# Values ahead of scores, projections and a feed-forward chunk moved into the loop, a new order at the end

## The chip, the core and the metric

One core of a Trainium2 chip runs the kernel, written instruction by instruction for each engine: TensorE (PE, matrix products), VectorE (DVE), ScalarE (ACT), GpSimd (POOL), and SyncE (SP), which here only issues DMA transfers. Each engine works through its own list in the order in which the program wrote it, and waits at semaphores for the others. The metric is the time of one execution on the device in microseconds (us), lower is better.

## The reference

Two sequences of 1024 tokens of 128 values go through one layer: local attention, a layer norm, a feed-forward block with ternary weights, a layer norm.

```python
qkv = xp @ w_qkv                       # 16 heads of 64; q scaled by 1/8
# token 0 ("bos") is a key of every query; its own output is its value row
# the other tokens stand in blocks of 16; a block of queries sees 5 blocks of
# keys (two before, itself, two behind), minus those that lie behind the query
sim  = einsum('bhnid,bhnjd->bhnij', qw, kw); sim = where(mask, -max, sim)
attn = softmax(sim)
attn = einsum('gh,bhnij->bgnij', w_th, attn)        # mixes the 16 heads
out  = einsum('bhnij,bhnjd->bhnid', attn, vw) ... @ w_out + b_out
x = layernorm(x + out)
h = gelu(ternary(w_up) applied to x / rms(x))       # 128 -> 512
x = layernorm(x + ternary(w_down) applied to h / rms(h))   # 512 -> 128
```

As the mask leaves only keys at or before the query, three blocks matter, so a query block has 50 keys: 3 x 17 less one.

## The kernel before

**Layout.** The 2 x 1024 tokens are cut into 8 chunks of 256 tokens. A chunk takes four slots of the main loop, `for s in range(STEPS)` with 32 slots, and each engine has its own copy of that loop. The weights were combined ahead, so that a query part is a product with the head's own matrix `Gh`/`Gl`, and the way out a product with `Mh`/`Ml`. A number of full precision is carried as a rounded high half and the rest, a low half (names ending in h and l, or high and low): ScalarE makes the high half, VectorE (or GpSimd) subtracts to get the low one, and three products (`split3`, L1106 to L1110) stand for one.

**The attention of a slot.** `queries(s, 0)` and `queries(s, 1)` (TensorE, 6 products of 256 columns each) make queries for the chunk ahead; ScalarE copies them out (`y_out`). `scores(s)` makes eight tiles of 50 keys (64 small products and a mask product). VectorE takes the maximum and subtracts it (`shift`), ScalarE makes the exponential, VectorE the sum and its reciprocal (`total`), GpSimd multiplies (`normalise`, L519). `transposes(s)` turns the result on TensorE, ScalarE and VectorE copy it out (`at_hi`, `at_lo`), `c_part(s)` multiplies by the values (12 products, L1257), `ct_hi` and `ct_lo` copy that out. `o_part(n, p)` is the projection of chunk n, in four parts of 12 products. In slot s the order on TensorE is: transposes(s-2), scores(s), pieces of feed-forward, queries(s, 0), one projection part (that of slot s-7), queries(s, 1), c_part(s-2). The lag of two slots is `LAG`, that of seven `O_LAG`.

**The feed-forward block** of chunk n is spread over slots by `ffn(s)`, which gives pairs (n, k) with k = s - FIRST[n], and FIRST[n] = 11 + 4n. k = -1: `stage` (ScalarE adds the bias to the attention's output); 0: `attn_back`, `residual`, `variance_roots`; 1: `input_scale`, `up_input`, `x1_T`, `x1_hi`; 2: `x1_lo`, `up`, `gelu`; 3: `hidden_high`; 4: `hidden_low` (GpSimd, L533), `squares`, `down`, `down_out`; 5: `down_back`, `square_sum`, `hidden_root`, `second_sum`; 6: `second_norm`, `last_root`; 7: `result_shift`; 8: `result`. Chunks 0 to 3 run so. Chunk 4 is in the loop up to `up` (at k = 4), and chunk 5 up to `attn_back`. All that is left stands behind the loop, in an order written out by hand for each engine, with the scores' last pieces, the projections of chunks 6 and 7, and the feed-forward work of chunks 4 to 7. `keep_busy(bank, count)` issues products whose result nobody reads.

**The window rows.** The values of a chunk are read from DRAM into `raw` by SP (`window`, 6 to 11 transfers). GpSimd rounds them into the high half (`rows_high(c)`, L502, waits until all of chunk c have landed) and subtracts for the low one (`rows_low`, L506), after which SP may overwrite `raw` with the next chunk's. In GpSimd's loop:

```python
for n, k in ffn(s):
    if k == 4 and n < 4: hidden_low(n, 0); hidden_low(n, 1)
    if k == 5: hidden_root(n)
normalise(s)
... # k == 0: variance_roots(n); k == 6: last_root(n)
if s % 4 == 1 and s < STEPS - 4: rows_high((s + 3) // 4)
if s % 4 == 0 and s > 0:         rows_low(s // 4)
```

## Time and profile before

| | |
|---|---|
| time, median of 3 runs | 241.5 us (241.25 to 242.36) |
| the profiled execution | 243.09 us, of it 241.3 us span of the profile |
| PE busy | 226.1 us, 94% of the span |
| DVE busy | 176.6 us, 73% |
| ACT busy | 164.1 us, 68% |
| POOL busy | 92.6 us, 38% |
| mean DMA traffic | 48 GB/s |
| granted PE clock | 9 tenths or more of full speed, in the last two of 40 slices 7 and 5 |

Busy time of an engine is the time in which it works on any instruction. Products overlap in the array, so the time of one (about 0.28 us) is more than its distance to the next (0.12 us); distances are read from start to start. In a row of a timeline stand the start and the duration in us, the engine, the line of the kernel, the operation, the output and input tiles with their sizes, how many instructions were merged, and in brackets how long the engine had been idle before and whom it waited for.

### The profile page before, as it was taken

The page shows a single profiled execution, that of the slowest core. Times are in us where ns is not written, and L with a number is a line of the kernel's source. Part 1 is how long each engine was busy: PE and PEld are TensorE (multiplying, and loading weights), DVE is VectorE, ACT ScalarE, POOL GpSimd, SP SyncE. Part 2 cuts the span into 40 slices and gives each one's busy share as a digit, 9 for nine tenths or more (in the row PEclk, how much of TensorE's full clock was granted, in tenths as well). Part 3 has the DMA queues.
Part 4 walks back from the last instruction along what each step waited for, and adds up shares of the span by engine and source line. Part 5 has one row for each costly group of instructions (what it writes and reads, how often), then busy time and mean ns, then how long its engine had stood idle before and what let it go on. Part 6 is the DMA issues. An engine that isn't in the chain of part 4 may idle for free.

```text
span 241.3 us, 10011 instructions
## 1 busy us (share of the span) xinstructions
PE 226.1 (94%) x4343; PEld 203.1 (84%) x4343; DVE 176.6 (73%) x461; ACT 164.1 (68%) x311; POOL 92.6 (38%) x111
## 2 busy tenths in 40 slices
PE   7999899999999999999999999999999989989970
PEld 7899789888999999888988998888988977889750
DVE  0674699987777882688766885688468999785864
ACT  2686466776666648985599559964898334988652
POOL 7035204531343342444515454536254353120542
PEclk9999999999999999999999999999999999999975
DMA  6937560020020001100200111010201001000002
GB/s 217 293 101 209 165 139 7 7 61 3 3 58 13 24 3 39 35 21 8 65 3 4 48 34 36 3 46 4 68 3 29 20 3 46 1 4 22 3 3 87
DMA packets 19107, 11.69 MB, mean 48 GB/s; under 512 B 2232, under 2 KB 18168, under 8 KB 18936
## 3 DMA queue, kind: packets, MB, share of 16 engines
q1 hardware_dynamic: 18324, 10.47, 15.3%
q8 instruction: 34, 0.56, 1.0%
q10 hardware_dynamic: 740, 0.59, 0.8%
q14 instruction: 9, 0.07, 0.1%
HBM read 8.91 MB, written 2.10 MB: 46 GB/s over the span
## 4 chain that ended last, share of the span: by engine, by line
PE 57%; DVE 15%; ACT 8%; issue 7%; POOL 6%; SPq 2%; DMA 2%; POOLq 0%; DVEq 0%; ACTq 0%
PE bank L1108 9%; PE bank L1110 8%; PE bank L1109 8%; PE bank L1257 7%; PE bank L1231 6%; PE bank L1215 4%; DVE CTl L876 4%; POOL gTl L533 2%; DVE AT L881 2%; POOL xw L506 2%; DMA raw<-in_L_attn_x 2%; SPq L395 2%; DVE sm L896 2%; PE bank L1327 2%; PE bank L1189 2%
## 5 line engine op out<-in xcount | busy, mean ns | idle before, releaser
L577 ACT ACTIVATE Yb<-bank 128x512 f32<-128x512 f32 x64 | 38.4, 601 | 28.4 <-PE bank L1110 27.9
L519 POOL TENSOR_TENSOR E<-E,rc 128x400 f32<-128x400 f32 x32 | 27.9, 871 | 77.3 <-DVE rc L898 77.3
L876 DVE TENSOR_TENSOR CTl<-bank,CTh 128x512 fp32r<-128x512 f32 x64 | 41.1, 683 | 22.3 <-ACT CTh L577 22.1
L1108 PE MATMUL bank<-xTh,Gh 128*128 128x256 f32 x128 | 39.4, 308 | 1.7 <-ACT Yb L577 1.5
L1108 PE MATMUL bank<-CTh,Mh 128*128 128x256 f32 x128 | 37.0, 289 | 0.6 <-DVE CTl L876 0.6
L577 ACT ACTIVATE CTh<-bank 128x512 fp32r<-128x512 f32 x64 | 34.8, 600 | 2.5 <-PE bank L1257 2.4
L1110 PE MATMUL bank<-CTh,Ml 128*128 128x256 f32 x128 | 36.1, 282 | 0.0
L724 ACT ACTIVATE E<-E 128x400 f32<-128x400 f32 x32 | 17.3, 541 | 27.5 <-DVE E L890 27.4
L1109 PE MATMUL bank<-CTl,Mh 128*128 128x256 f32 x128 | 36.0, 281 | 0.0
L1109 PE MATMUL bank<-xTl,Gh 128*128 128x256 f32 x128 | 35.8, 280 | 0.0
L1110 PE MATMUL bank<-xTh,Gl 128*128 128x256 f32 x128 | 35.7, 279 | 0.0
L1257 PE MATMUL bank<-AT,xw 50*128 50x256 f32 x384 | 31.1, 294 | 0.8 <-DVE AT L881 0.7
L1231 PE MATMUL bank<-xT,Yb 128*32 128x50 f32 x2048 | 29.9, 209 | 1.1 <-issue 1.1
L1231 PEld LDWEIGHTS bank<-xT,Yb 128*32 128x32 f32 x2048 | 25.2, 109 | 6.7 <-issue 6.4
L1257 PEld LDWEIGHTS bank<-AT,xw 50*128 50x128 f32 x384 | 24.6, 185 | 5.3 <-DVE AT L881 1.4
L896 DVE TENSOR_REDUCE sm<-E 128x8 f32<-128x400 f32 x32 | 18.2, 570 | 13.5 <-ACT E L724 13.4
L1108 PEld LDWEIGHTS bank<-xTh,Gh 128*128 128x128 f32 x128 | 24.3, 190 | 3.4 <-ACT Yb L577 2.3
L1108 PEld LDWEIGHTS bank<-CTh,Mh 128*128 128x128 f32 x128 | 24.1, 188 | 0.9 <-DVE CTl L876 0.9
L1109 PEld LDWEIGHTS bank<-xTl,Gh 128*128 128x128 f32 x128 | 24.2, 189 | 0.0
L1109 PEld LDWEIGHTS bank<-CTl,Mh 128*128 128x128 f32 x128 | 24.1, 189 | 0.0
L1110 PEld LDWEIGHTS bank<-xTh,Gl 128*128 128x128 f32 x128 | 24.1, 188 | 0.0
L1110 PEld LDWEIGHTS bank<-CTh,Ml 128*128 128x128 f32 x128 | 24.0, 188 | 0.0
(142 smaller groups left out, 469.3 us busy)
## 6 DMA issues: line engine op xcount, KB each, us to landing
raw<-in_L_attn_x SPq DMA_DIRECT2D x37, 64.0 KB
pt_rows<-PT SPq DMA_DIRECT2D x2, 512.0 KB, 4.7
R<-pt_rows SPq DMA_DIRECT2D x1, 1024.0 KB, 5.6
xr<-in_L_attn_x SPq DMA_DIRECT2D x6, 128.0 KB
out<-y SPq DMA_DIRECT2D x6, 128.0 KB, 1.9
raw<-in_L_attn_x SPq DMA_DIRECT2D x13, 56.0 KB
w_sb<-in_L_attn_w_qkv SPq DMA_DIRECT2D x2, 256.0 KB, 4.7
w_sb<-in_L_attn_w_qkv ACTq DMA_DIRECT2D x2, 256.0 KB, 4.5
```

The source lines that it names most:

```text
L395: sp.dma_start(raw[own, first:last, :], src[0:BLK]).then_inc(s_raw, 16)
L519: tt(e, e, rc[s % 2][:, :].unsqueeze(2).broadcast_to([P, TILES, WIN]), ALU.mult).then_inc(s_norm, 1)
L577: copy = lambda o, i, **k: nc.scalar.activation(o, i, ACT.Copy, **k)
L724: nc.scalar.activation(e, e, ACT.Exp).then_inc(s_exp, 1)
L876: v.tensor_tensor(ct_view(CTl[s // 4 % 2], s % 4, q), c_view(s, q), ct_view(f32(CTh[s // 4 % 2][:, :, :]), s % 4, q), ALU.subtract).then_i ...
L896: v.tensor_reduce(sm[k][:, :], E[k][:, :, 0:WIN], AX.X, ALU.add).then_inc(s_sum, 1)
L1108: mm(o, wh, rh, start=start, stop=False, **k)
L1109: mm(o, wh, rl, start=False, stop=False, **k)
L1110: return mm(o, wl, rh, start=False, stop=stop, **k)
L1215: ins = nc.tensor.transpose(o[:, :, IL * f:IL * f + IL], E[s % 2][:, k:k + 2, :].rearrange("p t w -> p (t w)"), ident[:, :])
L1231: mm(bank[S_BANK][lo:lo + 32, WIN * tile:WIN * tile + WIN], Yb[s // 4 % 2][:, ytile, lo:lo + 32], keys, start=(tile == 0), stop=False, ski ...
L1257: ins.append(mm(c_bank(s, q)[:, col], xw[s // 4 % 2][row, m, c, :], AT[row, a, col], start=(n == 0), stop=(n == 2)))
```

## The change

Six things, in all engines' lists:

1. From slot 8 on TensorE begins a slot with c_part(s-2), then scores(s), then transposes(s-1), one slot sooner than before. ScalarE and VectorE copy in that order. Slot 7 (`TURN`) is the slot in which the order turns.
2. O_LAG is 6: projection parts come one slot sooner. Slot 7 has two of them, and slot 31 too.
3. FIRST[n] is 10 + 4n for all chunks of the loop: every feed-forward stage of chunks 0 to 4 comes one slot sooner. The window rows keep their slots.
4. The square sums of a chunk stand inside the scores' block. Gelu stands ahead of the second query copy on ScalarE.
5. Chunk 4 runs in the loop up to second_sum, and its hidden_low is done by GpSimd and no longer by VectorE.
6. The lists behind the loop are new, and there are 30 idle products in place of 5.

```diff
@@ -56,7 +56,8 @@
...
 LAG = 2
-O_LAG = 7
+O_LAG = 6
+TURN = 7
 NT = B * N // P
...
@@ -279,19 +280,20 @@
...
-    if s < 28:
-        return [divmod(s - O_LAG, 4)] if s >= O_LAG else []
-    return {28: [(5, 1), (5, 2)], 29: [(5, 3)], 30: [(6, 0)], 31: []}[s]
-FIRST = [11 + 4 * n for n in range(5)] + [30]
+    if s < TURN:
+        return []
+    early = {7: [(0, 0), (0, 1)], 31: [(6, 1), (6, 2)]}
+    return early.get(s, [divmod(s - O_LAG, 4)])
+FIRST = [10 + 4 * n for n in range(6)]
...
-    return [(n, s - first) for n, first in enumerate(FIRST) if -1 <= s - first < (9, 9, 9, 9, 5, 1)[n]]
-UP_BANK = {5: (0, 2), 6: (0, 2), 7: (6, 5)}
+    return [(n, s - first) for n, first in enumerate(FIRST) if -1 <= s - first < (9, 9, 9, 9, 6, 1)[n]]
+UP_BANK = {5: (1, 0), 6: (2, 0), 7: (6, 5)}
 AT_BANK = {7: 5}
-XT_BANK = {5: 4, 7: 5}
+XT_BANK = {5: 2, 7: 5}
 DN_BANK = {5: 4, 6: 3, 7: 0}
...
@@ -309,14 +311,11 @@
...
-def c_bank(s, q):
-    return bank[(0, 2)[q] if s == 30 else C_BANK[q]]
 def y_bank(s, b):
...
 def squared(n):
-    return gT[0] if n < 4 else gT[2] if n % 2 else gsq
+    return gT[0] if n < 5 else gT[2] if n % 2 else gsq
...
@@ -343,7 +342,7 @@
...
 def c_view(s, q):
-    return c_bank(s, q)[:, :].rearrange("p (r h s) -> p r h s", r=2, s=BLK)
+    return bank[C_BANK[q]][:, :].rearrange("p (r h s) -> p r h s", r=2, s=BLK)
...
@@ -545,7 +544,7 @@
...
         for n, k in ffn(s):
-            if k == 4 and n < 4:
+            if k == 4:
                 hidden_low(n, 0)
...
@@ -561,11 +560,10 @@
...
+    last_root(4)
     variance_roots(6)
     variance_roots(7)
-    hidden_root(4)
     hidden_root(5)
-    last_root(4)
     hidden_root(6)
...
@@ -679,11 +677,11 @@
...
         o = slice(2 * t, 2 * t + 2)
-        if n < 4:
+        if n < 5:
             act.wait_ge(f_gl, 2 * n + t + 1)
...
             act.wait_ge(f_gl, 12)
-        elif n > 5:
+        elif n > 6:
             act.wait_ge(f_ss, n - 1)
...
@@ -705,24 +703,33 @@
...
             act.wait_ge(s_small, 32)
-        if s > LAG:
+        if LAG < s <= TURN:
             ct_hi(s - LAG - 1)
-        if 0 < s < O_LAG:
+        if 0 < s < TURN:
             y_out(s, 0)
-        if s >= LAG:
+        if LAG <= s <= TURN:
             at_hi(s - LAG)
-        if s == 0 or s >= O_LAG:
+        if s == 0 or s == TURN:
             y_out(s, 0)
-        if s < O_LAG:
+        if s >= TURN:
+            ct_hi(s - 2)
+            at_hi(s - 1)
+        if s > TURN:
+            y_out(s, 0)
+        if s < TURN:
             y_out(s, 1)
         for n, k in ffn(s):
-            if k == 4 and n < 4:
+            if k == 4:
                 squares(n, 0)
...
         nc.scalar.activation(e, e, ACT.Exp).then_inc(s_exp, 1)
-        if s >= O_LAG:
+        for n, k in ffn(s):
+            if k == 2:
+                gelu(n, 0)
+                gelu(n, 1)
+        if s >= TURN:
             y_out(s, 1)
...
@@ -730,46 +737,34 @@
...
         for n, k in ffn(s):
-            if k == 4 and n < 4:
+            if k == 4:
                 down_out(n)
...
                 x1_hi(n)
-            if k == 3 and n < 4:
+            if k == 3:
                 hidden_high(n, 0)
                 hidden_high(n, 1)
-            if k == 2 and n < 4:
-                gelu(n, 0)
-                gelu(n, 1)
-            if k == 8 and n < 3:
+            if k == 8:
                 result(n)
-    at_hi(30)
-    ct_hi(29)
-    gelu(4, 0)
+    x1_hi(5)
+    ct_hi(30)
     at_hi(31)
-    ct_hi(30)
-    gelu(4, 1)
+    stage(6)
     ct_hi(31)
-    x1_hi(5)
-    stage(6)
-    hidden_high(4, 0)
-    hidden_high(4, 1)
-    squares(4, 0)
-    squares(4, 1)
     gelu(5, 0)
...
     hidden_high(5, 1)
-    result(3)
     x1_hi(6)
+    result(4)
     squares(5, 0)
     stage(7)
+    squares(5, 1)
     gelu(6, 0)
...
     hidden_high(6, 1)
-    down_out(4)
-    squares(5, 1)
     down_out(5)
...
@@ -782,7 +777,6 @@
...
     down_out(7)
-    result(4)
     result(5)
...
@@ -1005,27 +999,25 @@
...
             dve.wait_ge(s_pt, 32)
-        if s > LAG:
+        if LAG < s <= TURN:
             ct_lo(s - LAG - 1)
-        if s >= LAG:
+        if LAG <= s <= TURN:
             at_lo(s - LAG)
+        if s > TURN:
+            ct_lo(s - 2)
+        shift(s)
+        if s == TURN:
+            ct_lo(s - 2)
         for n, k in ffn(s):
-            if k == 5 and n == 3:
+            if k == 5:
+                dve.wait_ge(f_back, n + 1)
                 hidden_sum(n)
+        if s >= TURN:
+            at_lo(s - 1)
         for n, k in ffn(s):
...
                 up_input(n)
-        shift(s)
-        for n, k in ffn(s):
-            if k == 5 and n < 3:
-                hidden_sum(n)
-            if k == 5 and n == 3:
-                second_sum(n)
-            if k == 6 and n == 3:
-                second_norm(n)
-            if k == 0 and n == 5:
-                residual(n)
         if s == STEPS - 1:
...
@@ -1035,11 +1027,11 @@
...
             ternary(0)
-        if 4 <= s < O_LAG:
+        if 4 <= s < TURN:
             fills(IN_STEP[s - 1][-1:])
...
         for n, k in ffn(s):
-            if k == 5 and n < 3:
+            if k == 5:
                 second_sum(n)
...
@@ -1055,45 +1047,39 @@
...
         for n, k in ffn(s):
-            if k == 0 and n < 5:
+            if k == 0:
                 residual(n)
-            if k == 6 and n < 3:
+            if k == 6:
                 second_norm(n)
-    at_lo(30)
-    ct_lo(29)
+    x1_lo(5)
+    ct_lo(30)
     at_lo(31)
-    ct_lo(30)
+    second_norm(4)
     ct_lo(31)
-    x1_lo(5)
     residual(6)
-    hidden_low(4, 0)
-    hidden_low(4, 1)
+    result_shift(4)
+    hidden_low(5, 0)
     input_scale(6)
     up_input(6)
-    hidden_low(5, 0)
     hidden_low(5, 1)
...
     input_scale(7)
-    hidden_sum(4)
     up_input(7)
-    second_sum(4)
+    hidden_sum(5)
     x1_lo(7)
-    hidden_sum(5)
-    second_norm(4)
     second_sum(5)
+    second_norm(5)
     hidden_sum(6)
     hidden_low(7, 0)
-    second_norm(5)
     hidden_low(7, 1)
-    result_shift(4)
     second_sum(6)
+    result_shift(5)
     hidden_sum(7)
     second_norm(6)
-    result_shift(5)
     second_sum(7)
...
@@ -1216,7 +1202,7 @@
...
-    def scores(s):
+    def scores(s, sums=()):
...
@@ -1230,6 +1216,9 @@
...
                    start=(tile == 0), stop=False, skip_group_check=True)
+        for n in sums:
+            pe.wait_ge(f_dS, n + 1)
+            square_sum(n)
         if s % (2 * SLOTS) == 0:
...
@@ -1242,10 +1231,7 @@
...
         pe.wait_ge(s_ATl, s + 1)
-        need(pe, s_CTl, 60 if s == 31 else 2 * s if s < 30 else 0)
-        if s == 30:
-            pe.wait_ge(s_sub, STEPS)
-            pe.wait_ge(s_Ye, 64)
+        need(pe, s_CTl, 2 * s)
         if s % 4 == 0:
...
@@ -1254,7 +1240,7 @@
...
                     row = slice(64 * q, 64 * q + WIN)
-                    ins.append(mm(c_bank(s, q)[:, col], xw[s // 4 % 2][row, m, c, :], AT[row, a, col],
+                    ins.append(mm(bank[C_BANK[q]][:, col], xw[s // 4 % 2][row, m, c, :], AT[row, a, col],
                                   start=(n == 0), stop=(n == 2)))
...
@@ -1272,10 +1258,8 @@
...
         pe.wait_ge(f_stage, n + 1)
-        if n < 5:
+        if n < 6:
             need(pe, f_gelu, 2 * n)
-        elif n == 6:
-            pe.wait_ge(f_gelu, 10)
         for i in range(CT):
...
@@ -1288,12 +1272,10 @@
...
-        if n < 5 and t == 0:
+        if n < 6 and t == 0:
             need(pe, f_y2, CT * n)
-        if n == 4 and t == 1:
-            pe.wait_ge(f_res, 6)
-        if n == 6:
-            pe.wait_ge(f_gelu, 11 + t)
+        if n == 6 and t == 1:
+            pe.wait_ge(f_gelu, 12)
         pe.wait_ge(f_xTl, n + 1)
...
@@ -1342,14 +1324,18 @@
...
     for s in range(STEPS):
-        if 0 < s < O_LAG:
+        if 0 < s < TURN:
             queries(s, 0)
...
             pe.wait_ge(s_evd, read_no("D", "p", 3))
-        if s >= LAG:
+        if LAG <= s <= TURN:
             transposes(s - LAG)
-        scores(s)
+        if s > TURN:
+            c_part(s - 2)
+        scores(s, [n for n, k in ffn(s) if k == 5])
+        if s > TURN:
+            transposes(s - 1)
         if s == FIRST[0]:
...
@@ -1358,21 +1344,21 @@
...
                 attn_back(n)
-            if k == 2 and n < 4 or k == 4 and n == 4:
+            if k == 2:
                 up(n, 0)
                 up(n, 1)
-        if s == 0 or s >= O_LAG:
+        if s == 0 or s >= TURN:
             queries(s, 0)
-        for n, k in ffn(s):
-            if k == 5:
-                square_sum(n)
-        if s == O_LAG:
+        if s == TURN:
             pe.wait_ge(s_eva, read_no("A", "m", 3))
...
             o_part(*part)
+            if part == (0, 0):
+                c_part(s - 2)
+                transposes(s - 1)
         for n, k in ffn(s):
-            if k == 4 and n < 4:
+            if k == 4:
                 down(n)
...
@@ -1380,41 +1366,38 @@
...
             fills(IN_STEP[s])
-        if s >= LAG:
+        if LAG <= s < TURN:
             c_part(s - LAG)
-    transposes(30)
-    o_part(6, 1)
+    x1_T(5)
     c_part(30)
     transposes(31)
-    o_part(6, 2)
+    o_part(6, 3)
     c_part(31)
-    x1_T(5)
-    o_part(6, 3)
+    up(5, 0)
+    up(5, 1)
     attn_back(6)
     o_part(7, 0)
-    up(5, 0)
-    up(5, 1)
     o_part(7, 1)
...
     up(6, 1)
+    down(5)
     attn_back(7)
-    down(4)
-    down(5)
-    down_back(4)
-    square_sum(4)
+    down_back(5)
+    square_sum(5)
+    keep_busy(1, 4)
     down(6)
-    down_back(5)
+    square_sum(6)
+    keep_busy(1, 4)
     x1_T(7)
-    square_sum(5)
     down_back(6)
+    keep_busy(1, 6)
     up(7, 0)
     up(7, 1)
-    square_sum(6)
-    keep_busy(2, 5)
+    keep_busy(1, 16)
     down(7)
...
```

## Rows read from the trace of the kernel before

**Rows 1.** Timeline of TensorE (PE), slots 14 and 15: start us, us, engine, line, operation, tiles.

```profile
97.65 0.38 PE L1108 MATMUL bank<-xTh,Gh 128*128 128x256 f32 x1 [0.36 <-ACT Yb L577]
...
98.55 0.97 PE L1257 MATMUL bank<-AT,xw 50*128 50x256 f32 x12
99.45 0.65 PE L1215 MATMUL bank<-ident,E 128*128 128x128 f32 x4
...
101.89 0.28 PE L1108 MATMUL bank<-CTh,Mh 128*128 128x256 f32 x1
...
103.32 0.28 PE L1309 MATMUL bank<-gTh,wdT 128*128 128x256 f32 x1
...
104.05 0.38 PE L1309 MATMUL bank<-gTh,wdT 128*128 128x256 f32 x1
```

**Rows 2.** Timeline of TensorE: scores(12), scores(28), the last values part.

```profile
82.06 0.92 PE L1231 MATMUL bank<-xT,Yb 128*32 128x50 f32 x64
...
185.08 0.92 PE L1231 MATMUL bank<-xT,Yb 128*32 128x50 f32 x64
...
209.61 0.98 PE L1257 MATMUL bank<-AT,xw 50*128 50x256 f32 x12
```

**Rows 3.** Timeline of TensorE at the end.

```profile
220.19 0.28 PE L1301 MATMUL bank<-x1Th,wuT 128*128 128x256 f32 x1
...
223.68 0.71 PE L1327 MATMUL bank<-ones,gsq 128*32 128x1 f32 x64
...
227.09 0.39 PE L1301 MATMUL bank<-x1Th,wuT 128*128 128x256 f32 x1
...
232.19 0.58 PE L1309 MATMUL bank<-gTh,wdT 128*128 128x256 f32 x1 [0.75 <-DVE gTl L949]
```

**Rows 4.** Busy time by stretches: us, then each engine, PEclk the granted clock.

```profile
230.00:241.30 11.30, 4.14 (x79) 3.10 (x78) 6.31 (x34) 4.25 (x10) 4.27 (x5) 0.58 0.16 48
```

**Rows 5.** Timeline of GpSimd (POOL), windows of chunks 4, 5 and 7.

```profile
87.76 0.86 POOL L519 TENSOR_TENSOR E<-E,rc 128x400 f32<-128x400 f32 x1 [4.27 <-DVE rc L898]
88.58 2.40 POOL L506 TENSOR_TENSOR xw<-raw,xw 114x1024 fp32r<-114x1024 f32 x1
...
99.62 1.04 POOL L502 CAST xw<-raw 114x1024 fp32r<-114x1024 f32 x1 [6.17 <-PE bank L1257]
...
101.45 2.55 POOL L533 TENSOR_TENSOR gTl<-gT,gTh 128x512 fp32r<-128x512 f32 x2
...
114.04 2.40 POOL L506 TENSOR_TENSOR xw<-raw,xw 114x1024 fp32r<-114x1024 f32 x1
...
119.77 0.69 POOL L544 TENSOR_TENSOR rstd<-var,exps 128x2 f32<-128x2 f32 x1
121.01 1.04 POOL L502 CAST xw<-raw 114x1024 fp32r<-114x1024 f32 x1 [0.55 <-DMA raw<-in_L_attn_x]
...
166.21 2.39 POOL L506 TENSOR_TENSOR xw<-raw,xw 114x1024 fp32r<-114x1024 f32 x1
...
175.10 1.04 POOL L502 CAST xw<-raw 114x1024 fp32r<-114x1024 f32 x1 [2.47 <-DMA raw<-in_L_attn_x]
```

**Rows 6.** Timeline of SyncE's queue, last issue of chunk 4's window.

```profile
97.54 0.70 SPq L398 DMA_DIRECT2D raw<-in_L_attn_x  x1
```

**Rows 7.** Timeline of VectorE (DVE) in a plain slot.

```profile
65.83 1.29 DVE L876 TENSOR_TENSOR CTl<-bank,CTh 128x512 fp32r<-128x512 f32 x2 [1.02 <-ACT CTh L577]
...
68.23 0.57 DVE L890 TENSOR_TENSOR E<-bank,mx 128x400 f32<-128x400 f32 x1
```

**Rows 8.** Timeline of ScalarE (ACT), the Gelu of chunk 0.

```profile
93.25 1.28 ACT L668 ACT_TABLE_LOAD   x1
94.55 1.09 ACT L668 ACTIVATE gT<-bank 128x512 f32<-128x512 f32 x2
```

**Rows 9.** Timeline of VectorE at the end.

```profile
231.44 0.69 DVE L949 TENSOR_TENSOR gTl<-gT,gTh 128x512 fp32r<-128x512 f32 x1
...
235.53 0.16 DVE L961 SCALAR_TENSOR_TENSOR weight<-hroot,ratio 128x2 f32<-128x2 f32 x1
```

## The prediction

> **What bounds the kernel now.** I read the page first. In its 40 slices TensorE shows 8 or 9 tenths everywhere but in the first and the last two. I went on to the waits of TensorE and of GpSimd, then to the timelines of both round one hidden-layer slot, and last to the end. I call one pass of the loop over s a slot, its eight score tiles scores(s), and so on. In the middle nearly everything is TensorE at a steady pace: a product of 256 columns every 0.117 us, 12 of them (one projection part) in 103.32 - 101.89 = 1.43, a values part in 99.45 - 98.55 = 0.90 [rows 1]. A plain slot is values 0.90, scores 0.9, four transposes 0.6 (0.66 with the last one's tail), projection 1.43 and two query parts of 6 products with a wait, 0.8 each: 5.4. Between scores(12) at 82.06 and scores(28) at 185.08 lie 103.02 us, four chunks of 25.8 [rows 2]. The reader is to see the two places in a chunk where TensorE waits: before the second query part of slot 14 (97.65, behind ScalarE's copy, 0.36 idle and about 0.5 between starts), and inside the down product of slot 15 (104.05, 0.26 lost and a slower first product, 0.36 together) [rows 1]. That is 0.9 us a chunk. The end is a chain: the last projection part ends at 220.19 where the products of up(6) start, those of up(7) start at 227.09, and the second half of down(7) at 232.19 has waited for VectorE [rows 3]; in that last stretch the granted clock is 0.58 on the mean [rows 4], so mostly at the lower of its two levels.
>
> **The other thing to see is GpSimd's queue.** GpSimd does three things in program order: normalise(s), the window rows (rows_low at s%4 = 0, rows_high at s%4 = 1), and hidden_low. After rows_low frees the raw buffer, SP issues the next window's transfers, and rows_high waits for the last. For chunk 4: rows_low ends at 88.58 + 2.40 = 90.98, the last issue starts at 97.54, rows_high starts at 99.62, 8.64 after the buffer came free [rows 5, 6]. (The row names a product as releaser, but that count was reached by the values part of slot 13; what is left is the last landing.) For chunk 5 it is 121.01 - 116.44 = 4.57; chunk 6 has as many transfers as 5, I give it the same. For chunk 7 it is 175.10 - 168.60 = 6.50 [rows 5]. None of it hurts before, because hidden_low comes two slots after rows_high's own slot (s = 15 against s = 13): rows_high(4) ends at 100.66, hidden_low starts at 101.45 [rows 5], the down product at 103.32 [rows 1].
>
> **The change, part by part.**
>
> *Work moved ahead.* At scores(28) TensorE has done more than before: one values part 0.90, one projection part 1.43, the transpose back and the square sums of chunk 3 (0.25, two transposes of the kind that take 0.66 in four, and 0.71, as at 223.68 [rows 3]), one x1 transpose with its wait 0.3. Together +3.6 at that point. It is no extra work; what it gives back stands under the end.
>
> *The loop's own waits.* In the new order a values part opens the slot, then come scores, then the transposes of the slot before. The risk is a ring: values, copy on ScalarE, ct_lo, the shift, at_lo on VectorE, next values. A pair of ct_lo takes 1.29, a shift piece 0.57 [rows 7]. I count 0.90 + 0.15 + 0.60 to the first copy's end, two ct_lo 1.2, two shift pieces 1.15, at_lo 0.68: 4.7 us in a slot of 5.4. So the plain slots stay TensorE's, with 0.7 to spare. Gelu in the slot s%4 = 0 now stands before the second query copy: its table load of 1.28 and 1.09 of Gelu [rows 8], and the load back for Exp in the slot after, push normalise(s) of that slot about 0.35 past the transposes. I take 0.35 a chunk, between 0 and 1.0 (the length of ScalarE's slack in either case). So 0.9 is removed and 0.35 put in its place: -0.55 a chunk, -2.2 for four.
>
> The Trainium skill (ScalarE: Activation LUTs, "What ACT_TABLE_LOAD costs") gives a switch of tables about 2.66 us, a drain counted in. Here the load starts at 93.25 and the Gelu at 94.55 [rows 8], so the trace shows 1.28 and no drain; by the page each slot with a load would be 1.4 longer, of which chunks 5 and 6 would feel about 0.35 each.
>
> *Hidden work one slot sooner.* FIRST goes from 11 to 10, so hidden_low(n) falls in the slot right after rows_high's, while rows_low and rows_high keep their slots. On GpSimd it stands behind rows_high, which stands behind a transfer. Count both from the end of normalise(12). TensorE: remaining 0.2, scores 0.9, transposes 0.6, queries 0.8, projection 1.43, queries 0.8; then values 0.9, scores 0.9, the 0.35, transposes 0.6, transpose back of attention 0.15, queries 0.8, projection 1.5: down(0) is wanted at 9.9 and done at 10.85. GpSimd: rows_low 2.40, transfer 8.64, rows_high 1.04, hidden_low 2.55 for two halves [rows 5], then half of down, 0.5: done at 15.1. TensorE is held 4.2. For chunks 5 and 6 last_root, which now stands ahead of rows_low and waits for second_norm, adds 0.85 (0.69 for itself [rows 5]): 0.85 + 2.40 + 4.57 + 1.04 + 2.55 + 0.5 = 11.9, held 1.05 each. For chunk 7, with 6.50: 13.85, held 3.0. Sum +9.3. ScalarE's squares wait for the same halves and Exp behind them, but the values, scores and squares that follow take longer than Exp, total and normalise (about 2.3), so nothing is added. Bounds: with chunk 5's interval in all four the sum is 3.4; if each hold also put one normalise (0.86) on the path it is 12.7. I take 9.3, the rows' own intervals.
>
> *Slots 28 to 31.* Without query parts the ring binds. It costs TensorE nothing where there was idle time before (about 2.4 us between 185 and 210.5), and the new order fills some of that. From scores(28) to the end of the last values part: before 209.61 + 0.9 - 185.08 = 25.4 [rows 2]; after, slot by slot with chunk 4's Gelu, down and squares in it, 25.7. So +0.3, between -1.5 and +2.5.
>
> *The end.* The last values part is now followed by up(5) and attn_back(6), which fit in the 2.1 us that the last ct_lo needs; before, the third part of chunk 6, held up behind it, made that 2.7, and up(5) stood inside the last projections: -1.55 to their end. Then up(6) and the new place of down(5) (0.94) stand before attn_back(7), +0.95. The idle products ahead of x1_T(7) and of up(7) have 4 and 6 of 0.117; squares and these come after down(6), and up(7) is late by another 1.45. From up(7) on it is the other way: low halves no longer wait for second_norm(5) (the one at 231.44 could be at 230.35, where its high half is done [rows 9]), the last products run at the upper clock, hidden_sum(7) comes 1.95 sooner after up(7), and so does all behind 235.53 [rows 9], less what it waits there for second_norm(6). Sum -1.55 + 0.95 + 1.45 - 2.0 = -1.15. Bounds -3.5 (idle products free) and +0.5.
>
> For the clock the Trainium skill (TensorE: Matmul & The Clock Gate, "Why this matters for your kernels") asks that TensorE not be left idle between bursts. By it the 16 products ahead of down(7) hold the upper level, as my sum has it; if they did not, the last part would be about 0.7 longer.
>
> *Everything else* (banks, squared into gT[0] for chunk 4, the square sums inside the scores block, removed special cases) is the same instructions in other places; the split of chunk 4 goes from VectorE (1.29 a pair) to GpSimd (2.55), in a slot without window rows: 0.
>
> **The sum.** +3.6 - 2.2 + 9.3 + 0.3 - 1.15 = +9.85. Against the profiled execution, 243.09 (span 241.3), that is 252.9; it lay 1.6 above the median 241.5, so for the median 251.3, said as 251.
>
> **Rivals.**
> *Half of the hold.* Landings come sooner, or TensorE is so late for other reasons in these slots that down(n) waits little: only chunk 4's and 7's holds stay, at half size, 3.6 instead of 9.3: 245.6. For it: the rows' intervals depend on SP's issue times (0.25 to 1.3 each), which vary. Against: the order on GpSimd is fixed, and 8.64 was measured. Chance 0.17.
> *Faster.* The hold does not show at all, and the new order takes every wait out of the loop (-3.6) while the end gains its full 3.5: 3.6 - 3.6 - 1.5 - 3.5 = -5 at most; half of that is likelier, 239. It decides if rows_high ends less than 5.4 us after rows_low in each chunk (10.4, when the second half of down is wanted, less 2.55 and 2.40). In the rows it is 9.7 for chunk 4, 5.6 for 5 and 7.5 for 7 (with last_root, 0.85 less is allowed). Chance 0.14.
> *Nothing.* Work and waits only change places; TensorE's products are the same but for 25 idle ones. The moved 3.6 is paid back by the end and the waits: 241.5. Chance 0.07.
> *Worse.* The ring binds in plain slots too, because ScalarE's copies come late: 0.3 in each of 20 slots, +6: 257. Against it: 0.7 to spare. Chance 0.07.
> The forecast has 0.55.
>
> **Numbers.** A measurement here tells 0.5% (1.2 us) from no change. Faster by more than that: 0.15. Within: 0.07. Slower: 0.78. The likeliest case alone is 248 to 254; with half the hold and its bounds taken in, 242 to 255, which leaves out the faster case and most of the worst one.
>
> **What would show it.** In the changed profile: in slots 14, 18, 22 and 26 TensorE waits before and inside down for gTl from GpSimd, about 3.5 and 1.3 for chunk 4; hidden_low starts right behind rows_high; waits for "gTl L533" sum to 8 us or more; scores(28) starts at about 196; the half clock is gone from the end. If hidden_low starts well after rows_high, and TensorE shows no such wait, the forecast is wrong, and so it is if the distance from scores(12) to scores(28) is under 104.

## The result

Median 259.36 us (258.06 to 262.54, 4 runs) against 241.93 for the kernel before, run beside it: 1.070 times as long, with an interval of 1.063 to 1.076. The forecast was 251.0, with a range of 242 to 255. The direction was right; the size was too small by 8 us, and the time lies above the whole range. Medians are of all executions; ratios and their intervals leave out the slow ones, here 262.54 with a mean granted clock of 0.938.

The page after, its span, PE and the granted clock (40 slices of 6.4 us):

```profile
span 257.4 us, 10064 instructions
...
PE 229.7 (89%) x4368; PEld 209.9 (82%) x4368; DVE 177.0 (69%) x459; ACT 168.2 (65%) x313; POOL 93.7 (36%) x113
...
PE   7999899999999996799969996999879969887890
...
PEclk9999999999999999799999999999958999999796
```

The reader is to see two things that the page before did not have: PE falls to 6 or 7 tenths in single slices of the loop, and PEclk has two dips inside the loop, the second to 5. They come in slots 14 and 26, where the down product of feed-forward chunk 0 or 3 follows the window rows of chunk 4 or 7. I name such a slot by its window: chunk 4's hold is slot 14, and those of chunks 5, 6 and 7 are slots 18, 22 and 26.

The first of TensorE's waits, after (engine, line, releaser: total us, times, longest us):

```profile
PE bank L1291 <- POOL gTl L532: 9.8, 7, 3.0
```

L1291 is the down product and L532 is hidden_low. TensorE stands 9.8 us behind the low halves that GpSimd makes; in the kernel before no such wait is in the list. TensorE at down(0), in chunk 4's hold, after:

```profile
100.48 0.28 PE L1096 MATMUL bank<-CTh,Ml 128*128 128x256 f32 x1
103.78 0.38 PE L1291 MATMUL bank<-gTh,wdT 128*128 128x256 f32 x1 [3.03 <-POOL gTl L532]
...
105.01 0.39 PE L1291 MATMUL bank<-gTh,wdT 128*128 128x256 f32 x1 [0.50 <-POOL gTl L532]
```

And GpSimd's queue, after, chunks 4, 5 and 7 (these answer to [rows 5]):

```profile
90.94 2.39 POOL L505 TENSOR_TENSOR xw<-raw,xw 114x1024 fp32r<-114x1024 f32 x1
96.83 0.86 POOL L518 TENSOR_TENSOR E<-E,rc 128x400 f32<-128x400 f32 x1 [3.50 <-DVE rc L892]
101.47 1.04 POOL L501 CAST xw<-raw 114x1024 fp32r<-114x1024 f32 x1 [3.78 <-DMA raw<-in_L_attn_x]
102.47 2.49 POOL L532 TENSOR_TENSOR gTl<-gT,gTh 128x512 fp32r<-128x512 f32 x2
...
121.87 2.41 POOL L505 TENSOR_TENSOR xw<-raw,xw 114x1024 fp32r<-114x1024 f32 x1
...
130.01 1.04 POOL L501 CAST xw<-raw 114x1024 fp32r<-114x1024 f32 x1 [2.21 <-DMA raw<-in_L_attn_x]
...
176.64 2.40 POOL L505 TENSOR_TENSOR xw<-raw,xw 114x1024 fp32r<-114x1024 f32 x1
...
185.81 1.04 POOL L501 CAST xw<-raw 114x1024 fp32r<-114x1024 f32 x1 [3.24 <-DMA raw<-in_L_attn_x]
186.81 2.50 POOL L532 TENSOR_TENSOR gTl<-gT,gTh 128x512 fp32r<-128x512 f32 x2
```

This is the chain that the forecast described: rows_high waits for the landing, hidden_low starts the moment rows_high is done (101.47 + 1.04 against 102.47), and the down product waits for its first half. What the forecast left out shows in the stretches of the kernel after (us, busy time of PE, PEld, DVE, ACT, POOL, then the granted clock, DMA share, GB/s):

```profile
84.92:105.80 20.88, 17.01 (x319) 15.65 (x318) 10.41 (x20) 14.68 (x26) 7.94 (x7) 1.00 0.08 22
105.80:109.20 3.40, 3.40 (x58) 2.95 (x60) 2.06 (x9) 1.87 (x5) 1.70 (x2) 0.50 0.15 43
...
187.70:194.50 6.80, 6.36 (x82) 5.62 (x86) 2.40 (x9) 4.29 (x9) 3.47 (x4) 0.50 0.05 14
...
200.08:225.99 25.91, 23.00 (x500) 21.00 (x498) 22.10 (x61) 18.16 (x33) 10.67 (x11) 1.00 0.07 18
...
238.90:242.30 3.40, 3.40 (x63) 3.16 (x56) 1.22 (x7) 0.06 (x1) 1.10 (x2) 0.50 0.02 5
```

Two of the four holds are followed by a stretch at 0.50, that is 1.2 GHz: 3.4 us behind chunk 4's (idle from 100.8 to 103.8; the clock fell at 105.8, 2 us after the products had begun again), 6.8 us from the end of chunk 7's on (idle 2.48, to 188.13). Between them, from 109.2 to 187.7, it is 1.00, over the holds of chunks 5 and 6. The milestones after, against [rows 2]:

```profile
84.92 0.92 PE L1217 MATMUL bank<-xT,Yb 128*32 128x50 f32 x64
...
200.08 0.92 PE L1217 MATMUL bank<-xT,Yb 128*32 128x50 f32 x64
...
225.09 0.97 PE L1243 MATMUL bank<-AT,xw 50*128 50x256 f32 x12
```

From scores(12) to scores(28) it is now 115.16 us where it was 103.02: 12.1 of the 16.1 us by which the span grew lie here. This distance is the yardstick of the experiments below.

### The profile page after: what moved, and what is told of

Same layout as the page of the kernel before. It is cut to its first block, busy times and chain, and to the rows that moved or that the text cites. A ratio compares the mean times of both kernels' runs of the same rounds, so it can differ in the third digit from the quotient of the medians.

```text
span 257.4 us, 10064 instructions
## 1 busy us (share of the span) xinstructions
PE 229.7 (89%) x4368; PEld 209.9 (82%) x4368; DVE 177.0 (69%) x459; ACT 168.2 (65%) x313; POOL 93.7 (36%) x113
## 4 chain that ended last, share of the span: by engine, by line
PE 49%; issue 15%; DVE 14%; POOL 14%; ACT 3%; SPq 2%; DMA 1%; POOLq 0%; DVEq 0%; ACTq 0%
PE bank L1094 7%; PE bank L1243 7%; PE bank L1217 6%; PE bank L1096 6%; PE bank L1095 6%; POOL xw L505 5%; POOL gTl L532 4%; DVE CTl L870 3%; PE bank L1201 3%; DVE sm L890 2%; POOL rstd L543 2%; PE bank L1175 1%; DVE AT L875 1%; PE bank L1149 1%; PE bank L1291 1%
## 5 line engine op out<-in xcount | busy, mean ns | idle before, releaser
L1096 PE MATMUL bank<-xTh,Gl 128*128 128x256 f32 x128 | 36.3, 283 | 0.0
L1243 PE MATMUL bank<-AT,xw 50*128 50x256 f32 x384 | 32.5, 303 | 3.0 <-DVE AT L875 2.9
L1243 PEld LDWEIGHTS bank<-AT,xw 50*128 50x128 f32 x384 | 25.8, 193 | 8.0 <-DVE AT L875 4.2
L1217 PE MATMUL bank<-xT,Yb 128*32 128x50 f32 x2048 | 30.7, 212 | 1.3 <-issue 1.3
L1217 PEld LDWEIGHTS bank<-xT,Yb 128*32 128x32 f32 x2048 | 26.0, 112 | 6.2 <-issue 3.0
L575 ACT ACTIVATE AT<-bank 128x512 fp32r<-128x512 f32 x32 | 19.6, 612 | 7.7 <-PE bank L1201 7.7
```

The source lines that it names most:

```text
L575: copy = lambda o, i, **k: nc.scalar.activation(o, i, ACT.Copy, **k)
L1096: return mm(o, wl, rh, start=False, stop=stop, **k)
L1217: mm(bank[S_BANK][lo:lo + 32, WIN * tile:WIN * tile + WIN], Yb[s // 4 % 2][:, ytile, lo:lo + 32], keys, start=(tile == 0), stop=False, ski ...
L1243: ins.append(mm(bank[C_BANK[q]][:, col], xw[s // 4 % 2][row, m, c, :], AT[row, a, col], start=(n == 0), stop=(n == 2)))
```

## The experiments

All ratios are to the kernel before, run on the same chip. A trace is one execution, and executions of one kernel differ: late_tail's ten, for example, have mean granted clocks from 0.967 to 0.983, and those at 0.967 to 0.974 took 244.2 to 245.5 us, the four at 0.981 to 0.983 took 242.3 to 243.0. So where a reading is about the clock, the clocks of all executions stand beside the trace.

**Window rows behind the hidden layer.** In the kernel after, rows_high of the same window moves one slot down, behind hidden_low and ahead of normalise:

```
-                if s % 4 == 1 and s < STEPS - 4:
-                    rows_high((s + 3) // 4)
 ...                                  # the loop part with hidden_low(n)
+                if s % 4 == 2 and s < STEPS - 4:
+                    rows_high((s + 2) // 4)
                 normalise(s)
```

> The changed kernel with one edit on GpSimd: rows_high(c) stands one slot later, behind hidden_low and ahead of normalise. Theory A (hidden_low is held behind rows_high, which waits for the window's transfers, and the half clock follows from TensorE's idle time): the wait of the down products for gTl of GpSimd, 9.8 us in the changed kernel, falls under 1 us, the stretches of half clock inside the loop go, scores(12) to scores(28) take 102 to 104 us instead of 115, and the time is 243 to 247 us. Rival B (the new order's ring over ScalarE and VectorE costs the time, GpSimd is only last): TensorE waits elsewhere for about as long, 255 us or more.

Measured: 244.36 us, ratio 1.007 (1.003 to 1.011); the distance from scores(12) to scores(28) came out below the 102 to 104 expected. No wait for gTl of GpSimd is left. First GpSimd's queue, then the stretch from scores(12) to scores(28), rows_late:

```profile
95.90 0.86 POOL L518 TENSOR_TENSOR E<-E,rc 128x400 f32<-128x400 f32 x1 [3.50 <-DVE rc L892]
96.71 2.55 POOL L532 TENSOR_TENSOR gTl<-gT,gTh 128x512 fp32r<-128x512 f32 x2
100.33 1.04 POOL L501 CAST xw<-raw 114x1024 fp32r<-114x1024 f32 x1 [1.06 <-DMA raw<-in_L_attn_x]
```

```profile
83.99:183.44 99.45, 97.84 (x2027) 90.74 (x2025) 75.00 (x201) 79.45 (x147) 46.17 (x44) 1.00 0.10 28
```

The stretch takes 99.45 us, all at full clock. So one order of two instructions costs 115.16 - 99.45 = 15.7 us in the loop, far more than the 9.3 that I gave it, and 15 us of the median. The order on GpSimd is shown to be the cause.

**The same wait with TensorE kept running.** In the kernel after, idle products stand where TensorE would be idle, about as many as fill the hold:

```
                     if k == 4:
+                        if n < 4:
+                            pe.wait_ge(f_gelu, 2 * n + 2)
+                            keep_busy(1, (26, 12, 12, 22)[n])
                         down(n)
```

> The changed kernel with idle products ahead of down(n), n = 0 to 3 (26, 12, 12, 22 of them, about as long as TensorE waits there). The hold on GpSimd stays. Theory A: the wait turns into idle products, the stretches of half clock at 106 to 109 and 188 to 194 us go, and with them 1.7 and 3.4 us of slow products: 253 to 256 us. Rival C (the half clock costs nothing, since the products run at half speed where TensorE waits anyway): 258 to 260 us.

Measured: 255.9 us, ratio 1.059 (1.053 to 1.065), 3.5 less than the kernel after, although nothing was taken out and 72 products were put in. The mean granted clock of its four executions is 0.969 to 0.984; the four of the kernel after have 0.938 to 0.965. First the stretch from scores(12) to scores(28), then the filled wait of chunk 4, fill_wait:

```profile
83.42:194.74 111.32, 107.85 (x2099) 99.71 (x2097) 74.81 (x201) 80.32 (x147) 46.18 (x44) 1.00 0.09 25
```

```profile
99.09 3.27 PE L1317 MATMUL bank<-wuT 128*128 128x256 f32 x26
102.45 0.39 PE L1291 MATMUL bank<-gTh,wdT 128*128 128x256 f32 x1
```

The down product still starts when GpSimd lets it, but the clock is 1.00 all through. This splits the 15.7 in two: 111.32 - 99.45 = 11.9 is the hold in fill_wait, and 115.16 - 111.32 = 3.8 is what the kernel after adds. The 3.8 is not all clock. 2.6 of it lie in the slots of chunks 4 and 7 and the ones behind them, where the kernel after has its stretches at 0.50. The other 1.2 lie in the slots of chunks 5 and 6, at 1.00 in both kernels, where GpSimd in fill_wait got its rows sooner:

```profile
126.87 1.04 POOL L501 CAST xw<-raw 114x1024 fp32r<-114x1024 f32 x1 [1.83 <-DMA raw<-in_L_attn_x]
...
153.27 1.04 POOL L501 CAST xw<-raw 114x1024 fp32r<-114x1024 f32 x1 [1.12 <-DMA raw<-in_L_attn_x]
```

From rows_low's end to rows_high's start it took 5.37 and 4.65 there, and 5.73 and 5.62 in the kernel after; for chunks 4 and 7 it was the other way, 8.28 and 7.22 against 8.14 and 6.77. With its own intervals the kernel after would hold for 0.7 longer than fill_wait, about 12.6, which leaves about 3.1 for the lower clock. Both are estimates from two traces.

**Windows not fetched.** The kernel after without the transfers of the windows of chunks 1 to 7 (those chunks compute with chunk 0's rows), so that rows_high has nothing to wait for:

```
             def next_window(c):
                 sp.wait_ge(s_xwl, c)
-                window(*divmod(c, 2))
...
-                pool.wait_ge(s_raw, landed(c))
+                pool.wait_ge(s_raw, landed(0))
```

> The changed kernel without the window transfers of chunks 1 to 7: the value rows of chunk 0 serve all chunks, so the transfers are left out of the computation; GpSimd's order and work are the same. Theory A with the landing as its cause: rows_high starts at once behind normalise, the hold falls to under 1 us, 243 to 247 us. Rival D (the order on GpSimd alone, 2.4 + 1.0 + 2.6 us of work in a row, holds down): 3 us or more of wait for gTl stay and the time is 248 us or more.

Measured: 246.01 us, ratio 1.018 (1.014 to 1.021). GpSimd at chunk 4, no_window:

```profile
96.15 0.86 POOL L517 TENSOR_TENSOR E<-E,rc 128x400 f32<-128x400 f32 x1 [3.50 <-DVE rc L891]
96.96 1.04 POOL L500 CAST xw<-raw 114x1024 fp32r<-114x1024 f32 x1
97.96 2.55 POOL L531 TENSOR_TENSOR gTl<-gT,gTh 128x512 fp32r<-128x512 f32 x2
```

The order is that of the kernel after, and yet the hold is gone: scores(12) to scores(28) takes 100.57, 1.1 more than rows_late. So the landing is what holds; of the work of rows_high, 4 x 1.04, about 1.1 shows. The missing transfers also make this kernel lighter on DMA (36 GB/s on the mean in place of 45). That does not explain its time: rows_late has all the transfers and is no slower.

**The hold alone, in the kernel before.** Only the two window-row calls move by a slot, so that rows_high comes directly ahead of hidden_low; nothing else of the change is in it:

```
-                if s % 4 == 1 and s < STEPS - 4:
-                    rows_high((s + 3) // 4)
-                if s % 4 == 0 and s > 0:
+                if s % 4 == 2 and s < STEPS - 4:
+                    rows_high((s + 2) // 4)
+                if s % 4 == 1 and s > 1:
                     rows_low(s // 4)
```

> The kernel before with rows_low and rows_high one slot later each (s%4 = 1 and 2), nothing else: the old order gets the same distance between rows_high and hidden_low as the changed kernel has. Theory A: down waits for gTl of GpSimd by 1 to 4 us per chunk, some 8 us in sum, half clock in the loop in places, 249 to 256 us. Rival E (the hold needs the new order on TensorE, which asks for down sooner): under 3 us more, at most 245 us.

Measured: 257.2 us, ratio 1.056 (1.046 to 1.065), 1 us above what was expected. The first of TensorE's waits and two stretches, before_rows_later:

```profile
PE bank L1309 <- POOL gTl L533: 8.8, 7, 4.1
```

```profile
106.50:113.30 6.80, 5.01 (x26) 4.49 (x26) 2.00 (x8) 2.56 (x5) 4.26 (x5) 0.50 0.04 13
195.30:205.50 10.20, 10.20 (x169) 8.95 (x168) 7.49 (x26) 3.79 (x9) 2.56 (x3) 0.50 0.10 27
```

From scores(12) at 82.80 to scores(28) at 198.45 it is 115.65, near the kernel after's 115.16. The nearness is in part luck: this trace is of the longest of the four executions (253.3 to 259.5), with 17 us at 0.50. But the shortest is still 11.6 above the kernel before. The hold and its half clock need no other part of the change than where the window rows stand. One wait of 1.2 us is new beside them: a values part waits for rows_low, which moved too.

**The end: order alone.** rows_late is still no faster than before, with an end of 243.6 - 183.4 = 60.2 us behind scores(28) (before: 56.2) in its trace, which is one of its two longest executions (245.37 of 241.7 to 245.6). The first try moves only the attention's transposes of chunk 7 ahead of chunk 5's down product, to have ScalarE's copy under it:

```
-            down(5)
             attn_back(7)
+            down(5)
             down_back(5)
```

> rows_late (244.4 us) with attn_back(7) ahead of down(5) again, as in the kernel before. Theory F (the end is a chain from attn_back(7) on, and down(5)'s 0.94 us stands in it): 0.9 us less, 243.5 us. Rival G (TensorE waits 2 us behind attn_back(7) for ScalarE's copy of down(5) anyway, so the order of these two is worth nothing): 244.4 us.

Measured: 244.4 us, ratio 1.008 (1.005 to 1.011): no gain over rows_late. The other side's expectation held.

**The end: also without idle products.** On top of it the 4 + 4 + 6 idle products ahead of x1_T(7) and up(7) go, and square_sum(6) stands behind x1_T(7):

```
             square_sum(5)
-            keep_busy(1, 4)
             down(6)
+            x1_T(7)
             square_sum(6)
-            keep_busy(1, 4)
-            x1_T(7)
             down_back(6)
-            keep_busy(1, 6)
             up(7, 0)
```

> The same, and without the 4 + 4 + 6 idle products ahead of x1_T(7) and up(7), square_sum(6) behind x1_T(7). Theory F (they and down(6) and square_sum(6), at half clock, hold up x1_T(7), whose input is ready 3 us sooner): 4 us less than rows_late, 240.5 us. Rival H (they pay, since without them the clock is at its half level for longer): 244 us or more.

Measured: 240.79 us, ratio 0.995 (0.993 to 0.998), 3.6 less (3.1 by the ratios). The same stretch in late_tail, then in late_tail_free:

```profile
225.40:232.20 6.80, 6.05 (x88) 5.41 (x87) 2.09 (x12) 0.66 (x2) 0.95 (x3) 0.50 0.01 2
```

```profile
225.40:232.20 6.80, 6.14 (x143) 5.26 (x132) 4.81 (x23) 4.95 (x11) 2.06 (x3) 1.00 0.01 2
```

TensorE ran 143 products in this stretch instead of 88, and up(7) starts at 226.06 instead of 231.23. Both kernels wait 1.42 us for ScalarE's copy ahead of down_back(5); only in late_tail's trace does a stretch at 0.50 follow. These traces are far apart by luck as well: late_tail's is its longest execution (clock 0.969 of 0.967 to 0.983), late_tail_free's has the highest clock of its ten (0.987 of 0.974 to 0.987). Two more kernels take the two halves of this edit apart.

**Only the idle products out.** late_tail without its three calls of keep_busy ahead of up(7), the order kept:

```
-            keep_busy(1, 4)    # ahead of down(6)
-            keep_busy(1, 4)    # ahead of x1_T(7)
-            keep_busy(1, 6)    # ahead of up(7)
```

> late_tail without its 4 + 4 + 6 idle products ahead of down(6), x1_T(7) and up(7); square_sum(6) stays ahead of x1_T(7). Theory K (the idle products make the lower clock: the chip counts what stood before them, and they only push real work into the low stretch): no stretch at 0.50 between 223 and 233, and the median at 240.8 to 241.6, like late_tail_free (240.79). Rival L (the place of square_sum(6), 0.7 us of 1-column products ahead of the transposes, is what matters): a stretch at 0.50 from about 225 on, only the 1.6 us of the products saved, 242.8.

Measured: 242.78 us, ratio 1.004 (1.001 to 1.006): the rival's 242.8. By the medians the idle products account for 1.6 us, their own 14 x 0.117; by the ratios it is 1.0, and each ratio is good to about 0.7 us. The lower clock is there without them: 0.968 to 0.980 over ten executions, late_tail 0.967 to 0.983. TensorE, tail_no_idle:

```profile
225.18 1.03 PE L1309 MATMUL bank<-ones,gsq 128*32 128x1 f32 x64
226.14 0.69 PE L1270 MATMUL bank<-ident,x1n 128*128 128x128 f32 x2
227.58 0.69 PE L1299 MATMUL bank<-ident,dS 128*128 128x128 f32 x2 [0.75 <-ACT dS L575]
```

**Only four idle products in.** late_tail_free with one call more:

```
             square_sum(5)
+            keep_busy(1, 4)
             down(6)
```

> late_tail_free with 4 idle products ahead of down(6) and nothing else. Theory K: the lower clock comes back behind 225, median 242.5 to 244. Rival M (it takes more than these four, or the order): they cost their own 0.47 us at most, 241.0 to 241.3, clock 1.00 until up(7).

Measured: 240.52 us, ratio 0.993 (0.990 to 0.995). Theory K's 242.5 to 244 did not come, and the products cost even less than the 0.47 of the other side (241.0 to 241.3). But in the trace the clock was not 1.00, as that side had it: it is at 0.50 from 223.4 to 226.8, for 3.4 us. Over all ten executions the mean clock is 0.981 to 0.987, in none lower than late_tail_free's lowest (0.974). TensorE, tail_four_idle:

```profile
225.59 0.63 PE L1270 MATMUL bank<-ident,x1n 128*128 128x128 f32 x2
226.14 0.92 PE L1309 MATMUL bank<-ones,gsq 128*32 128x1 f32 x64
226.99 0.44 PE L1299 MATMUL bank<-ident,dS 128*128 128x128 f32 x2
```

With the square sums behind x1_T(7) they cover ScalarE's copy, and the second wait (0.75 in late_tail and in tail_no_idle) is gone. So the 3.6 us are, by the medians, 1.6 of idle products and 2.0 of order. In the 2.0 are the second wait and the lower clock. Executions of like mean clock tell them apart roughly: at 0.973 to 0.975 tail_no_idle took 242.8 on the mean (7 executions) and late_tail_free 241.6 (3), so about 1.2 us of the order are there at an equal clock, and about 0.8 go with the clock. That is an estimate from few executions.

**Slot 29 filled.** rows_late waits 1.98 us for the last link of the ring (the shifted attention of VectorE) ahead of a values part at 193.08, and the clock is at 0.50 from 193.2 to 196.6. 16 idle products in that gap, on rows_late:

```
                     if part == (0, 0):
                         c_part(s - 2)
+                    if s == 29:                    # ahead of the two lines above
+                        pe.wait_ge(s_Ye, 64)
+                        keep_busy(2, 16)
```

> rows_late with 16 idle products in slot 29, where TensorE waits 2 us for at_lo ahead of its values part (Gelu and the table loads of slot 28 hold ScalarE). Theory J (that wait lets the clock fall in slots 29 to 30, 3.4 us at half level in the profile): the stretch goes, 1.5 us less, 243 us. Rival K (the clock is kept or lost by the end's own waits): no change, 244.4 us.

Measured: 241.86 us, ratio 0.999 (0.997 to 1.001), 2.5 less than rows_late by the medians and 1.9 by the ratios. Slot 29, late_fill, and the stretch round it:

```profile
191.21 2.07 PE L1317 MATMUL bank<-wuT 128*128 128x256 f32 x16
193.35 0.97 PE L1243 MATMUL bank<-AT,xw 50*128 50x256 f32 x12
```

```profile
190.00:200.00 10.00, 9.93 (x216) 9.26 (x218) 7.90 (x17) 9.04 (x18) 6.08 (x5) 1.00 0.01 2
```

The values part starts 4.92 behind scores(28) (188.43), without them 4.93, and the stretch behind it runs at 1.00: the same exchange as in fill_wait, with a gain 0.4 to 1.0 us larger than expected. It is the clock that gives it: late_fill's ten executions have 0.983 to 0.991, rows_late's 0.967 to 0.982, and rows_late's three at 0.982 took 241.7 to 242.6, as long as late_fill's.

**Both together.** rows_late with slot 29 filled, attn_back(7) first, 14 idle products in the wait ahead of down_back(5), none ahead of down(6), x1_T(7) and up(7), and square_sum(6) behind x1_T(7).

> All of it: rows one slot later, 16 idle products in slot 29, attn_back(7) ahead of down(5), 14 idle products in the wait for ScalarE's copy of down(5) in place of the 4 + 4 + 6 ahead of x1_T(7) and up(7). If both terms are right, full clock to the last up product and 238 to 239.5 us, faster than the kernel before by 1%; if the end is bound elsewhere, 242 us.

Measured: 239.69 us, ratio 0.991 (0.988 to 0.994). It beats the kernel before by 0.9% and the kernel after by 7.6%, and is 0.2 us above the 238 to 239.5 expected. The gains do not add: it is 4.7 under rows_late, where slot 29 and the end alone gave 2.5 and 3.6. One stretch from slot 28 to up(7), late_fill_tail:

```profile
187.00:226.00 39.00, 36.55 (x666) 33.82 (x665) 29.59 (x95) 27.59 (x53) 14.10 (x14) 1.00 0.06 16
```

## Why the prediction was wrong

The direction and the mechanism of the hold held; the sum was 6.25 us short in the profiled execution (257.4 against 241.3 + 9.85 = 251.15). The other 1.8 of the 8 come from the step to the median: I took off 1.6, by which the profiled execution of the kernel before lay above its median, and after it lay 0.2 below. Point by point:

**The hold: right place, its intervals too short.** The forecast gave +9.3 by 4.2, 1.05, 1.05 and 3.0. fill_wait shows the holds without their clock, slot by slot against rows_late: 4.26, 2.15, 1.44 and 4.00, together 11.9; with the intervals of the kernel after it is about 12.6. So the term was 2.6 to 3.3 short. Of the 3.3, 2.0 are the interval from rows_low's end to rows_high's start. After it is 8.14, 5.73, 5.62 and 6.77 (26.3 in all; chunk 5: 130.01 - 124.28), and I had 8.64, 4.57, 4.57 and 6.50 (24.3) from [rows 5]. It was not chunk 5's row taken for chunk 6: in the kernel before chunk 6 has 4.68 (142.44 to 147.12). The interval of the same chunk differs between kernels and executions, 4.6 to 5.7 for chunks 5 and 6, and I took it for fixed. Why it differs stays open. The bound of 12.7 held.

**The failed step: a wait priced at its length alone.** The rest of the loop's miss is the lower clock behind the holds, a term that the sum put at nothing without a reason: 2.6 at least, about 3.1, and 3.8 at most (115.16 less fill_wait's 111.32). I had read the granted clock of 0.58 at the end [rows 4] and spoken of idle TensorE there, and did not ask what four waits of up to 3 us would do to the same clock in the middle. The half clock in the loop was no named case of mine, neither as a term nor as a bound. The Trainium skill (TensorE: Matmul & The Clock Gate, "Why this matters for your kernels") says that TensorE should not be left idle between bursts. The runs agree: with the holds filled by products nobody needs the median is 3.5 us lower. I cited that section for the end and did not carry it to the holds.

**The loop's own pace: better than I thought.** Without holds scores(28) stands at 183.44 (rows_late) against a forecast of 185.08 + 3.6 - 2.2 = 186.5; with the 0.93 by which the kernel after is later at scores(12), it is 184.4, 2.1 better. Part of it is a gain that I did not see: four transposes cost less where they now stand, 0.58 from start to next start in a plain slot before (70.48 to 71.06) and 0.36 after (69.22 to 69.58):

```profile
69.15 0.24 PE L1226 MATMUL bank<-mask,sel 128*128 128x136 bf16 x1
69.22 0.60 PE L1201 MATMUL bank<-ident,E 128*128 128x128 f32 x4
69.58 0.37 PE L1094 MATMUL bank<-xTh,Gh 128*128 128x256 f32 x1
```

The values part, the scores, the mask product and the transposes together take 2.37 before (69.58 to 71.95) and 2.18 after (67.40 to 69.58), 0.19 a slot less; over 16 slots that would be 3.0, an estimate.

So the loop's account closes. The hold with its clock is 15.7, 6.4 more than the 9.3, and -2.1 + 6.4 = +4.3, and scores(28) lies at 200.08 against 195.8 (185.08 + 3.6 - 2.2 + 9.3).

**Slots 28 to 31: right.** 25.7 forecast from scores(28) to the end of the last values part, 25.91 measured.

**The end: wrong sign.** Forecast -1.15, so 29.6 from there to the end; measured 257.40 - 225.99 = 31.4 (+1.8), 0.6 more than before. The two terms that I took off came out: from the end of the last values part to up(6) it is 8.16 where it was 9.68 (-1.5; forecast -1.55), and from up(7) to the end 12.05 where it was 14.21 (-2.2; forecast -2.0, although the low half that I let start at 230.35 found VectorE busy with the first one until 230.65 in the trace). The miss lies between up(6) and up(7). Ahead of down_back(5) TensorE waits for ScalarE's copy, and behind that the clock is at 0.50 from 238.9 to 242.3:

```profile
236.00 0.38 PE L1264 MATMUL bank<-ident,attnS 128*128 128x128 f32 x2
237.97 0.44 PE L1299 MATMUL bank<-ident,dS 128*128 128x128 f32 x2 [1.59 <-ACT dS L575]
...
238.99 1.22 PE L1317 MATMUL bank<-wuT 128*128 128x256 f32 x4
240.01 0.41 PE L1291 MATMUL bank<-gTh,wdT 128*128 128x256 f32 x1
...
245.35 0.29 PE L1283 MATMUL bank<-x1Th,wuT 128*128 128x256 f32 x1
```

The reader is to see the products of down(6) at 0.41 instead of 0.28. Up(7) starts 11.2 behind the start of up(6) (234.15), where before it was 6.9 [rows 3]; my terms there (down(5) and 1.45) made 9.3: 1.9 short, the whole of the end's miss. The runs on rows_late show what part of it can be had back: 3.6 us of the median, 1.6 for the idle products and 2.0 for square_sum(6) ahead of x1_T(7), the lower clock in it, where I charged 1.45 in all.

**What I said would show it.** The waits for gTl sum to 9.8 (8 or more said); chunk 4's are 3.03 and 0.50 in the list, 3.2 and 0.65 between starts (3.5 and 1.3 said, half right); hidden_low does start right behind rows_high; scores(28) is at 200.1 and not at 196. The half clock did not go from the end, and is now in the loop as well.

**The rivals.** Half of the hold and the faster case had a condition on rows_high ending soon after rows_low. It was not met: 9.2 us for chunk 4, 7.8 for chunk 7. With rows_high behind hidden_low (rows_late, 244.4) the first of them, 245.6, would have been near; the faster case's 239 would not. The ring in plain slots, my 257, has the time nearest to the measured one and the wrong mechanism: plain slots are 5.2 us and not 5.7.

## What to carry to other kernels

Before moving a step one slot sooner, look at what stands ahead of it in its own engine's queue and at the DMA that this one waits for: a queue in program order passes a landing's lateness on to work that needs nothing of it. Price an idle stretch of TensorE at its length and then add the stretch at the lower clock that may follow, here about 3 us for two stretches. One trace does not show which of two kernels keeps the clock: set the mean clocks of all their executions side by side. And put idle products into the wait itself; ahead of work that is ready they cost their own time (14 of them 1.0 to 1.6 us) and, here, kept no clock up.

## What the runs showed of the hardware

- The lower clock does not follow every idle stretch of TensorE of one length. In the trace of the kernel after, the waits of 3.03 and 2.48 are followed by 3.4 and 6.8 us at 0.50, those of 1.45, 1.33 and 1.97 (slot 29) by none; in that of rows_late the wait of 1.98 in slot 29 is followed by 3.4. Of the four traces with the same wait of 1.42 ahead of down_back(5), two have 6.8 us at 0.50 behind it, one 3.4 and one none, though what precedes the wait is the same code. It differs between executions of one kernel too: rows_late's ten have mean clocks of 0.967 (four), 0.974 to 0.976 (three) and 0.982 (three). What decides that stays open.
- The four transposes take 0.58 us from start to next start between a values part and the scores (before) and 0.36 between the mask's small bf16 product and a query product (after). Both neighbours changed, so these rows do not say which of them matters, nor why.
